# Counts turned into runs: two ScalarE copies and a scan over 16-bit halves in place of a VectorE shift

## The reference

```
xn = _layernorm(x)
support = xn @ weight
msgs = edge_weight[:, None] * support[dst]
agg = segment_sum(msgs, src, num_segments=6250)
x = x + relu(agg + bias + xn) + mix(xn)
x = x + experts(_layernorm(x))
```

## Time and profile before

| what | us |
|---|---|
| median of 3 runs | 3291.57 |
| lowest and highest | 3285.41, 3292.38 |
| the profiled execution | 3286.34 |
| its span, first to last instruction | 3284.6 |

### The profile page before, as it was taken

One profiled execution on the slowest core, in us unless ns is written; L12 is line 12 of the kernel. 1 busy time (PEld: TensorE's weight loads), 2 busy tenths in 40 slices (PEclk: granted clock), 3 DMA queues, 4 the chain that ended last, 5 costly groups with the idle time before them and its releaser, 6 DMA issues.

```text
span 3284.6 us, 41743 instructions
## 1 busy us (share of the span) xinstructions
PE 2569.4 (78%) x10366; PEld 1957.5 (60%) x10366; DVE 2112.8 (64%) x4939; ACT 1237.0 (38%) x2686; POOL 2194.4 (67%) x2116
## 2 busy tenths in 40 slices
PE   5899998667777776876877876867868765799998
PEld 2777776545455454554655555645646554688887
DVE  7988998745555656666676576676576567666521
ACT  1111111044444443433433433434434351455533
POOL 0455655677777777777777777777777774556654
PEclk9666666589998887988988978989879886799999
DMA  3111113064444543453454444444444438456542
GB/s 118 31 31 31 32 31 101 7 135 119 124 118 120 116 115 117 116 129 117 117 128 120 116 119 126 118 117 115 125 116 109 117 111 275 139 133 149 108 95 43
DMA packets 418592, 353.19 MB, mean 108 GB/s; under 512 B 253830, under 2 KB 359884, under 8 KB 418252
## 3 DMA queue, kind: packets, MB, share of 16 engines
q0 software_dynamic: 106672, 244.73, 27.9%
q1 hardware_dynamic: 303212, 98.01, 13.3%
q10 hardware_dynamic: 8496, 8.09, 0.7%
HBM read 285.06 MB, written 60.91 MB: 105 GB/s over the span
## 4 chain that ended last, share of the span: by engine, by line
PE 30%; DVE 26%; DVEq 9%; issue 8%; DMA 3%; POOL 2%; ACT 1%; POOLq 0%; SPq 0%; ACTq 0%
DVE R L1597 13%; PE ps L952 8%; DVEq L1588 7%; PE ps L1026 5%; PE ps L1018 5%; PE ps L1142 4%; PE ps L1130 4%; DMA out<-y_w,zt 2%; DVEq L1597 2%; DVE is_low L1584 1%; DVE xnT L1657 1%; PE ps L986 1%; DVE stats L1501 1%; PE ps L969 1%; POOL out L824 1%
## 5 line engine op out<-in xcount | busy, mean ns | idle before, releaser
L782 POOL DMA_INDIRECT rows<-support,t_dst x1624 | 1582.3, 974 | 503.1 <-issue 457.2
L952 PE MATMUL ps<-rows,hot 128*128 128x256 f32 x3248 | 910.2, 435 | 369.8 <-DVE R L1597 352.5
L1597 DVE TENSOR_TENSOR R<-R,ps 128x256 f32 x1624 | 683.1, 421 | 710.1 <-PE ps L952 254.9
L952 PEld LDWEIGHTS ps<-rows,hot 128*128 128x128 f32 x3248 | 690.5, 220 | 584.2 <-issue 327.2
L1258 ACT ACTIVATE hot<-is_low,t_w 128x128 f32<-128x128 bf16 x1624 | 689.2, 513 | 174.3 <-DVE is_low L1584 160.2
L756 POOL DMA_INDIRECT slots<-rec,st_pos x224 | 313.2, 1398 | 330.9 <-issue 157.9
L896 PE MATMUL ps<-spread,piece 128*104 128x64 bf16 x1568 | 302.4, 369 | 27.9 <-DVE spread L1494 27.9
L896 PEld LDWEIGHTS ps<-spread,piece 128*104 128x104 bf16 x1568 | 302.3, 286 | 34.1 <-DVE spread L1494 30.7
L824 POOL DMA_INDIRECT out<-y_w,zt x112 | 177.0, 1580 | 176.8 <-DVE y_w L1921 95.9
L1142 PE MATMUL ps<-w_all,h_t 128*128 x896 | 207.6, 386 | 1.9 <-DVE y_w L1921 1.9
L1130 PE MATMUL ps<-zt_t,w_sel 128*128 128x256 f32 x896 | 205.5, 383 | 1.9 <-ACT zt_t L1337 1.9
(11 more groups left out here) (267 smaller groups left out, 2889.8 us busy)
## 6 DMA issues: line engine op xcount, KB each, us to landing
rows<-support,t_dst POOLq DMA_INDIRECT x1624, 2.7
zt<-routed SPq DMA_DIRECT2D x56, 268.0 KB, 2.8
xa<-in_x SPq DMA_DIRECT2D x24, 512.0 KB
w_all<-in_L_ffn_W SPq DMA_DIRECT2D x16, 512.0 KB, 10.3
R<-zeros SPq DMA_DIRECT2D x1, 6400.0 KB, 27.1
xin<-in_x SPq DMA_DIRECT2D x12, 512.0 KB
support<-sup_sb ACTq DMA_DIRECT2D x12, 512.0 KB, 3.0
xf<-in_x SPq DMA_DIRECT2D x12, 512.0 KB
```

The costliest lines, as they stand in the source:

```text
L782: pool.indirect_dma_start(out=rows[h][:, j, :], out_offset=None, in_=support, in_offset=bass.IndirectOffsetOnAxis(ap=t_dst[a][:, col:col + ...
L952: last = pe.matmul(ps[q][:, t * D:(t + 1) * D], lhsT=hot[o][:, q * 2 + t, :], rhs=rows[h][:, q * 2 + t, :], start=True, stop=True)
L1597: dve.tensor_tensor(out=there, in0=there, in1=ps[q][:, t * D:(t + 1) * D], op=ALU.add).then_inc(carried, 1)
```

## The change

`count(q)` now copies the counts in two steps. The first multiplies by 1/16 and adds 15/32, as float32, and raises a new semaphore `parted`. ScalarE waits for that and adds 2^23 to `nrun` in place, after which the low bits of the float's word are the rounded number of runs. VectorE's shift and its wait are gone; the scan reads `nrun` as 16-bit integers, every second one, which are the low halves of the words. `nrun` becomes float32, its leading column is still zero, and VectorE's count of chained instructions in a pair falls from 36 to 34.

```
-SORT_SEQ = 36
+SORT_SEQ = 34
+WHOLE = float(1 << 23)
...
-        nrun = alloc(sorting, "nrun", [P, CH, NB + 1], I32)
+        nrun = alloc(sorting, "nrun", [P, CH, NB + 1], F32)
...
                 act.activation(nrun[:, :, 1:NB + 1], ps[0][:, 0:NB * CH].rearrange("p (b c) -> p c b", c=CH), ACT.Copy,
-                               bias=float(RUN - 1)).then_inc(counted, 1)
+                               bias=(RUN - 1) / (2.0 * RUN), scale=1.0 / RUN).then_inc(parted, 1)
+                act.wait_ge(parted, q + 1)
+                act.activation(nrun[:, :, 1:NB + 1], nrun[:, :, 1:NB + 1], ACT.Copy, bias=WHOLE).then_inc(counted, 1)
...
                 dve.wait_ge(counted, q + 1)
-                seq(dve.tensor_scalar(out=nrun[:, :, 1:NB + 1], in0=nrun[:, :, 1:NB + 1], scalar1=RUN.bit_length() - 1,
-                                      scalar2=None, op0=ALU.logical_shift_right), apart=True)
                 dve.tensor_tensor_scan(out=first[:, :, :].rearrange("p c b -> p (c b)"),
                                        data0=fresh[:, :, :].rearrange("p c b -> p (c b)"),
-                                       data1=nrun[:, :, :].rearrange("p c b -> p (c b)"), initial=0.0, op0=ALU.mult, op1=ALU.add)
+                                       data1=nrun[:, :, :].bitcast(I16).rearrange("p c (b h) -> p (c b) h", h=2)[:, :, 0], initial=0.0, op0=ALU.mult, op1=ALU.add)
```

More of the change, by code:

```diff
@@ L409, in program @@
         v_read = sem("v_read")
+        parted = sem("parted")
         counted = sem("counted")
@@ L734, in _ @@
             pool.memset(fresh[:, :, 0:1], 0.0)
-            pool.memset(nrun[:, :, 0:1], 0)
+            pool.memset(nrun[:, :, 0:1], 0.0)
             for s in range(STREAMS):
```

## The result

The changed kernel takes 3293.55 us (median of 20 runs) against 3288.94 us for the kernel before (also 20): a ratio of 1.0016, with a 95% interval of 1.0010 to 1.0022, so some 5.3 us more. That is slower, as the interval leaves out 1, but by less than the 0.2% that the prediction had set as its bound; it had given this outcome 0.49 and a loss above the bound 0.44. The forecast was + 5.7 us. The forecast level, 3297 us, lies 3.5 us too high, and 2.6 of that is its base: the three runs that it started from had a median of 3291.57.

The account below looks back on a forecast made before the run. TensorE, waiting only for ScalarE, was taken to bound the sort up to 519 us, VectorE its end. + 0.2 + 7.5 + 0 - 2.0 = + 5.7 us on 3286.34 gives 3292.0, on the runs' median 3297 us; range 3289 to 3304.

Parts of the forecast that it names:

- What bounds the sort: Sort, 94 to 519 us: TensorE plus its waits for ScalarE fill 425.0 us; rival VectorE sets the pace, chance 0.05.
- The second copy's price: ScalarE's count ahead of `xn`: first `xn` starts 0.68 us later, bounds 0.50 to 0.85.
- the gap of 3.3 to 3.4 us that was to show the step: TensorE's idle time ahead of the transposes, eleven times, instead of 2.70 us.
- Eleven times 0.68 = 7.5 us: Even batches 2 to 22: the transposes begin 0.68 us later each time, + 7.5 us.
- a term that could be 4.7 us either way: TensorE's clock at the ranks matmuls: 4.7 us more or less; rivals: gives back 0.17, clock or odd batches add 0.15.
- Odd batches at nothing: Third product behind the odd batch's count and `take`: hidden by 0.1 us, costed at nothing; 2 us if cover fails.
- The first batch: `normalise(0)`: second copy puts it back 0.68 us, the absent shift gives 0.50 back, + 0.2 us.
- The end of the sort: Batches 24 to 27, VectorE is the path: 4 x 0.50 saved, - 2.0 us.
- The scan: VectorE's scan over 16-bit halves: stays at 0.99 us; rival, slower by 0.42 us, + 7.4 us in all, chance 0.05.
- VectorE's wait at `place`: VectorE's wait for TensorE's sort: up from 18.6 us to some 37.
- a longer gap could only cost: Idle ahead of the transposes, by the skill's clock rule: nearer to + 10 than + 5.7 us; kept as a rival only.

Follow-up runs that it names:

- the copy alone: Kernel before, shift kept, plus a second ScalarE copy of nrun into a spare tile before counted is raised: ratio 1.0022.
- the second copy moved: Changed kernel with only the second copy of even batches moved behind normalise, the first staying ahead: ratio 0.9995.
- the kernels above: Kernel before plus ScalarE copies ahead of counted: one of 8 elements 1.0027, one whole 1.0022, two 1.0030, three 1.0065.
- two copies: Kernel before, shift kept, with two more whole ScalarE copies of nrun into spare tiles ahead of counted: ratio 1.0030.
- the kernel with one copy: Kernel before with one ScalarE copy that scales and rounds, writing int32, and no VectorE shift: ratio 0.9989.

## Why the prediction was right, step by step

- **What bounds the sort.** Right, and shown: TensorE's waits in the changed kernel, the copy alone (+ 7 us with VectorE's work untouched), the shift's absence alone (- 3.6 of 14 us), and the second copy moved (loss gone, ScalarE's work the same).
- **The second copy's price.** The mechanism was right, the size off. 0.68 us had a wait gap of 0.18 in it, read off a DMA issue behind a copy. Between two activations it is 0.03 us. The copy is 0.53 us long, as forecast (0.52). 0.97 - 0.40 = 0.57 us more on ScalarE, 0.49 in TensorE's gap, as the count begins 0.04 us behind the recorded end of the ranks where it was 0.11; the lower bound of 0.50 was just missed, and so was the gap of 3.3 to 3.4 us that was to show the step.
- **Eleven times 0.68 = 7.5 us.** The sum came out at 7.6 for two reasons that cancel. The gap took 10 x 0.49 = 4.9 us of the 7.05 by which the ten steps grew. The other 2.1 us are the clock: no step of 38.5 us is left. The prediction had this as a term that could be 4.7 us either way and took zero for it. It was not zero. Its two directions both came: the two short steps grew by 2.4 and 2.5 us, of which the gap is 0.49, and the other eight, 40.7 us on average, grew by less than the gap, to 40.9. And the kernels above show it is not even a separate term: from a gap of 2.87 to one of 3.61 us the step is 41 us, whatever the gap. That the sum agrees to 0.1 us at the last large transposes is luck.
- **Odd batches at nothing.** Right for this change: TensorE has no wait there. The cover was 0.1 us, and two copies break it.
- **The first batch.** + 0.1 measured, + 0.2 forecast.
- **The end of the sort.** The stall of batch 22 shrank from 5.85 to 5.32 us and the step through it gave 1.0 us back, which was not forecast; that of batch 23 grew from 2.83 to 3.72, and the step through it took 0.3. Of the four savings of 0.50 us, three came (0.51 each) and the last went into a wait for a scatter, 0.75 us. Together - 2.1 us instead of - 2.0, which is luck as well. That the clearing of R is what holds these scatters up was argued from the order in time; no run leaves it out.
- **The scan.** 0.98 us, as the rows of before had it: 16-bit input altered nothing. Over int32 words, without a shift ahead of it, it is 0.98 us too (the kernel with one copy). The Trainium skill (DVE: opcode table, instruction layouts, handler registers and perf-mode slots, section "Datapath and trigger behaviour") says that the built-in scan feeds its result back and runs at half throughput; that the operand's type then doesn't matter was the prediction's inference, and the 0.98 us agree with it.
- **VectorE's wait at `place`.** 28.0 us where some 37 were foreseen; the rest is in the waits for scatters, which rose from 1.7 to 12.8 us. VectorE comes to its store positions earlier, and finds the scatters not landed.

## What to carry to other kernels

Shifting work from one engine to another is priced by what stands behind it in the new engine's queue: here half a microsecond that nobody on the path needed was paid eleven times because the path's own work stood behind it. Ask of each instruction in a queue what it waits for, not only how long it takes: the count cost 0.40 us ahead of `normalise`, but its wait for TensorE cost 2.70, and moving it by one place made the kernel 0.7% faster and the very change that had lost 5 us win 7 to 9, for 0.9% in all. And two busy shares of 90% say nothing of which engine is the bound; the table of waits does.

## What the runs showed of the hardware

- ScalarE's second activation, waiting for a semaphore that the first raises, starts 0.03 us after its end, against 0.15 us between two instructions on VectorE (shift and scan). The price of a chained pair on ScalarE is close to the sum of the two durations.
- Rounding: a ScalarE copy with scale 1/16 and bias 15/32 that writes int32 gives the count of runs rounded to the nearest, so neither 2^23 nor a shift is needed.
- The step of a TensorE stream that changes between 1.2 and 2.4 GHz doesn't grow in proportion to its gap: 40.2 us at a gap of 2.70, 41 at 2.87, 3.19 and 3.61, 42.0 at 4.03. The Trainium skill (TensorE: Matmul & The Clock Gate, "What's actually happening") says that activity lifts the lower rate. The runs agree in that 30 of the 33 large sets of transposes without a gap take 1.04 to 1.07 us, and nearly all behind one 1.5 to 1.97. What the prediction read out of it, that a longer gap could only cost, is not what the ranks show: with a gap of 3.61 us they are 0.84 us a pair shorter than with 3.19, and the step, once settled, is as long as with 2.87.
